# Batch statistics from second moments of the features, summed in the main loop

## The chip, the cores and the metric

The kernel runs on one core of a Trainium2 chip. The time is the device time of one execution in microseconds (us). The time before is the median of three runs. Five engines are named: PE (TensorE, matrix products), DVE (VectorE), ACT (ScalarE), POOL (GpSimd) and SP (SyncE, which here only issues transfers). Each takes its instructions in the order in which they are written, and waits at a semaphore until the count it asks for is reached; everything behind a waiting instruction on the same engine waits with it.

## The reference

The program takes x and ctx, both 32 x 128 x 1024. Four blocks follow each other: two chunked attentions with a layer norm, a graph block over the 30 nearest neighbours, and a third attention with a layer norm. Only the graph block matters here, cut to its first batch norm:

```python
idx = _knn(x_loc, k)                       # 30 neighbours of each of 32 x 1024 points
rel = pts[bidx, idx] - pts[:, :, None, :]
...                                        # rho, theta, phi: a radius and two angles
sph = jnp.stack([rho, theta, phi], axis=-1)
feat = jnp.concatenate([sph, sph - jnp.mean(sph, axis=-1, keepdims=True)], axis=-1)
lrelu = lambda h: jax.nn.leaky_relu(h, 0.2)
h = lrelu(_bn(feat @ W1.T, g1, b1))        # 6 channels, mean and variance over all rows
h = lrelu(_bn(h @ W2.T, g2, b2))           # 3 channels
h = lrelu(_bn(h @ W3.T, g3, b3))           # 1 channel
att = jax.nn.softmax(h[..., 0], axis=-1)
```

The first layer is linear in the three features, so its mean and variance over all 983,040 rows follow from the features' mean and their 3 x 3 matrix of second moments.

## The kernel before

There are three stages, one after the other, with a barrier between them.

**The main loop** (`attention_and_neighbours`) takes 32 batches in 24 steps each: 768 steps, and a tail of 48 steps in which only lagging work is left. In step s, PE makes the scores SC of step s (L581, L586), projections PJ for the next pass, distances PD (L599, L600), then the transposes PT of step s-3 (L607), the weighted values OP of step s-4 (L615), and fetches G of neighbours' coordinates (L558). DVE takes the scores' maximum (L1046), then reciprocals, and in pieces the search of neighbours: MAX8, MATCH_REPLACE8 and FIND_INDEX8 over rows of 1024. ACT makes the exponentials `prob` (L722) and copies PT and OP from PSUM (L729, L735). POOL divides `prob` by its sum (L835), splits rows (L813 to L823), masks and adds (L853, L860), selects coordinates (L924 to L927) and does the features of one batch (L937 to L977).

A second batch runs behind the first: everything with a name in `..._AT` happens so many steps after that batch's last step of attention, once in 24 steps. `ROOT_AT` is the radius on ACT (`sides`), `TURN_AT` and `SPH_AT` are the last steps of the two angles on POOL (L964; L975 and L977), and `SPH_OUT_AT` is the store of the three features by SP (L503, L505). The features of a batch are 128 partitions x 256, of which every 32nd and 31st partition are padding.

PE's scores of step s need ACT's exponentials of step s-2, since SC has two buffers:

```python
pe.wait_ge(exped, at_least(i, START + i * STEPS + s - 1, START))
```

**The batch norms** (`batch_norms`) load the features of all batches into `S` and run over them three times. In the first pass PE makes the first layer Z of each piece (L1258), and DVE takes its statistics (L1402):

```python
for y in range(2 * PIECES):
    dve.wait_ge(z1_ready, y + 1)
    dve.bn_stats(st1[:, y % 2, y // 2, :], Z[0:ROWS, y % BANKS, :]).then_inc(z1_read, 1)
```

PIECES is 60, so that is 120 products and 120 statistics. After it come an aggregate, two small products that average over the rows (`across`), an inverse root on POOL and `gain` and `shift`. The second pass makes the first layer again, for ACT to scale and shift it (L1327). `SERIAL` numbers the links of this chain.

**The weighted sum** (`neighbour_sum`) is not touched.

## Time and profile before

| | us |
|---|---|
| median of three runs | 6317.76 |
| lowest and highest | 6315.41, 6318.28 |
| the profiled execution's own time | 6316.55 |
| its span | 6314.8 |

| engine | busy, us | share of the span |
|---|---|---|
| PE | 5517.6 | 87% |
| DVE | 5699.2 | 90% |
| ACT | 4499.4 | 71% |
| POOL | 3397.5 | 54% |

The span begins with the main loop, which ends at about 4634 us; the batch norms end at about 5060 us. A share of busy time says which engine is full on average, not which wait ends last: that is read from the rows of a stretch in order of time. The trace shows a float32 product as two passes of PE (120 products are 240 rows), and a transpose as one.

### The profile page before, as it was taken

The page shows a single profiled execution, that of the slowest core. Times are in us where ns is not written, and L with a number is a line of the kernel's source. Part 1 is how long each engine was busy: PE and PEld are TensorE (multiplying, and loading weights), DVE is VectorE, ACT ScalarE, POOL GpSimd, SP SyncE. Part 2 cuts the span into 40 slices and gives each one's busy share as a digit, 9 for nine tenths or more (in the row PEclk, how much of TensorE's full clock was granted, in tenths as well). Part 3 has the DMA queues.
Part 4 walks back from the last instruction along what each step waited for, and adds up shares of the span by engine and source line. Part 5 has one row for each costly group of instructions (what it writes and reads, how often), then busy time and mean ns, then how long its engine had stood idle before and what let it go on. Part 6 is the DMA issues. An engine that isn't in the chain of part 4 may idle for free. (4 is left out here: it accounts for less than half of the span.)

```text
span 6314.8 us, 227176 instructions
## 1 busy us (share of the span) xinstructions
PE 5517.6 (87%) x82516; PEld 3384.3 (54%) x82516; DVE 5699.2 (90%) x8045; ACT 4499.4 (71%) x17145; POOL 3397.5 (54%) x3375
## 2 busy tenths in 40 slices
PE   7888888888888888888888888888669859999999
PEld 3555555555555555555555555555433347777776
DVE  7999999999999999999999999999855687777786
ACT  7888888888888888888888888888604623333333
POOL 3466666666666666666666666666620033333332
PEclk9999999999999999999999999999879979999999
DMA  2333333333333333333333333333340023333332
GB/s 45 95 105 97 99 98 96 95 95 107 98 110 91 99 98 96 97 97 109 96 107 93 97 97 97 97 108 92 106 108 0 0 64 89 94 87 88 84 94 74
DMA packets 651349, 568.72 MB, mean 90 GB/s; under 512 B 553072, under 2 KB 574832, under 8 KB 616208
## 3 DMA queue, kind: packets, MB, share of 16 engines
q1 hardware_dynamic: 613264, 284.51, 19.2%
q10 hardware_dynamic: 36864, 268.45, 12.0%
q8 instruction: 702, 11.50, 0.8%
q14 instruction: 519, 4.25, 0.2%
HBM read 384.76 MB, written 67.24 MB: 72 GB/s over the span
## 5 line engine op out<-in xcount | busy, mean ns | idle before, releaser
L722 ACT ACTIVATE prob<-SC,row_max 128x64 f32<-128x64 f32 x6144 | 1842.2, 337 | 389.7 <-DVE row_max L1046 381.6
L835 POOL TENSOR_TENSOR prob<-prob,row_rec 128x512 f32<-128x512 f32 x768 | 830.2, 1082 | 1433.5 <-DVE row_rec L1054 1403.5
L722 ACT ACTIVATION_READ_ACCUMULATOR prob<-SC,row_max 128x1 f32 x6144 | 1393.0, 230 | 0.0
L1038 DVE FIND_INDEX8 nbr<-top,dist 128x8 uint16<-128x1024 f32 x1024 | 1234.4, 1217 | 0.0
L1031 DVE MAX8 top<-dist 128x8 f32<-128x1024 f32 x1024 | 1190.8, 1203 | 1.7
L1033 DVE MATCH_REPLACE8 dist<-top,dist 128x1024 f32<-128x1024 f32 x768 | 923.3, 1206 | 0.0
L586 PE MATMUL SC<-k_bd,q_t 128*64 128x256 f32 x6144 | 907.1, 420 | 0.0
L1697 ACT ACTIVATE dense<-DM 128x512 f32<-128x512 f32 x512 | 305.6, 597 | 747.0 <-PE DM L1656 746.7
L607 PEld LDWEIGHTS PT<-ident,prob 128*128 128x128 f32 x3072 | 361.7, 145 | 833.8 <-issue 815.6
L1805 DVE TENSOR_TENSOR d_oh_a<-lo,iota_a 128x4096 bf16<-128x4096 bf16 x256 | 583.9, 2291 | 239.7 <-PE DM L1656 239.1
L607 PE MATMUL PT<-ident,prob 128*128 128x128 f32 x3072 | 490.9, 284 | 351.0 <-ACT prob_t L729 350.3
L558 PE MATMUL G<-table,low_all 128*128 128x24 bf16 x24576 | 706.0, 174 | 66.1 <-ACT picked L748 32.8
L558 PEld LDWEIGHTS G<-table,low_all 128*128 128x128 bf16 x24576 | 667.4, 97 | 177.5 <-issue 94.6
L1656 PEld LDWEIGHTS DM<-placed,d_oh_a 128*128 128x128 bf16 x24576 | 645.8, 96 | 111.4 <-issue 77.4
L1656 PE MATMUL DM<-placed,d_oh_a 128*128 128x32 bf16 x24576 | 651.4, 177 | 31.1 <-DVE d_oh_a L1805 28.2
L1046 DVE TENSOR_REDUCE row_max<-SC 128x8 f32<-128x512 f32 x768 | 518.6, 675 | 73.7 <-PE SC L586 73.3
L586 PEld LDWEIGHTS SC<-k_bd,q_t 128*64 128x64 f32 x6144 | 395.5, 144 | 316.5 <-issue 217.2
L600 PE MATMUL PD<-ctx 128*128 128x512 f32 x1024 | 542.1, 611 | 0.0
L729 ACT ACTIVATE prob_t<-PT 128x512 f32<-128x512 f32 x768 | 498.7, 649 | 0.4 <-PE PT L607 0.3
L1634 PE MATMUL AG<-dense,x_t 128*128 128x512 f32 x1024 | 476.5, 608 | 0.9 <-issue 0.7
L715 ACT ACTIVATE dist<-PD,xcol 128x512 f32<-128x512 f32 x512 | 372.1, 727 | 127.2 <-PE PD L600 111.2
L536 PE MATMUL PJ<-ctx,w_in 128*128 128x512 f32 x768 | 438.3, 653 | 0.1
(187 smaller groups left out, 9475.7 us busy)
## 6 DMA issues: line engine op xcount, KB each, us to landing
low_all<-low_scratch ACTq DMA_DIRECT2D x256, 1024.0 KB, 5.0
k_bd<-k_t SPq DMA_DIRECT2D x3072, 16.0 KB, 1.9
placed<-compact SPq DMA_DIRECT2D x256, 192.0 KB, 3.8
ctx<-in_ctx SPq DMA_DIRECT2D x32, 512.0 KB, 6.2
mask<-in_mask SPq DMA_DIRECT2D x32, 512.0 KB, 8.7
xb<-in_x SPq DMA_DIRECT2D x32, 512.0 KB, 3.3
x_scratch<-xb SPq DMA_DIRECT2D x32, 512.0 KB, 6.9
y_scratch<-y_b SPq DMA_DIRECT2D x32, 512.0 KB, 6.6
```

The source lines that it names most:

```text
L558: last = pe.matmul(G[:, g * 24:(g + 1) * 24], hot[:, t % 2, col:col + 128], table[:, v % BPB, part, :], start=(part == 0), stop=(part == 2))
L586: last = pe.matmul(bank[64 * ch:64 * ch + 64, cols], q_t[:, w % 2, here], k_bd[:, s // 2 % KEY_BUFS, s % 2 * 2 + ch, cols], start=False, s ...
L600: pe.matmul(PD[:, :], ctx[:, u, t * 128:(t + 1) * 128], ctx[:, u, h * HALF:(h + 1) * HALF], start=False, stop=True).then_inc(pd_ready, 1)
L607: last = pe.transpose(PT[:, m * 128:(m + 1) * 128], prob[:, r % 4, m * 128:(m + 1) * 128], ident[:, :])
L722: last = act.activation(prob[:, s % 4, g * CHUNK:(g + 1) * CHUNK], SC[:, s % 2, g * CHUNK:(g + 1) * CHUNK], ACT.Exp, bias=row_max[:, s % 2 ...
L835: pool.tensor_tensor(pr, pr, row_rec[:, r % 2, :].unsqueeze(2).to_broadcast([128, 8, CHUNK]), ALU.mult).then_inc(normed, 1)
L1031: dve.max(best, row).then_inc(top_step, 1)
L1033: dve.match_replace(row, best, row, NEG_BIG).then_inc(top_step, 1)
L1038: last = dve.max_index(nbr[:, uu % BPB, t, k * 8:(k + 1) * 8], best, row)
L1046: dve.tensor_reduce(row_max[:, s % 2, :], SC[:, s % 2, :].rearrange("p (h k) -> p h k", h=8), AX.X, ALU.max, negate=True).then_inc(maxed, 1)
L1656: last = pe.matmul(DM[:, x % DM_BANKS, (g % 16) * 32:(g % 16 + 1) * 32].rearrange("p (q m) -> p q m", q=4), oh_a[:, t % 2, g, :], placed[: ...
L1805: dve.tensor_tensor(oh_a[:, t % 2, :, :].rearrange("p g (a two) -> p g a two", two=2), lo2[:, u, t, :, :].unsqueeze(2).to_broadcast(wide), ...
```

## The change

It moves the first batch norm's statistics into the main loop.

- POOL writes `centred` for each batch (`CENTRE_AT` = 46): the three features side by side in 8 strips of 96 columns with a column of ones behind them; the radius has a typical value taken off, and padding rows are zero. That is a copy and three TENSOR_SCALAR instructions. It takes the space of `r2m`.
- PE adds to the 96 x 97 block `GR` in PSUM, over all batches, the product of each strip with itself: 8 float32 products in each batch (`GRAM_AT` = 47), ahead of OP in the same step. PE waits for `centre_ready` there. ACT copies the sum to SBUF once, at the end.
- `TURN_AT` goes from 45 to 44, `SPH_AT` from 46 to 45, and `SPH_OUT_AT` from 47 to 46. The radius is stored by itself, 39 steps behind, and SP loads one value of it into all partitions (`typical`, 42 steps behind).
- ACT waits for `centre_ready` of the batch before at the root, and POOL for `gram_ready` of the batch before at L948. Two POOL instructions lose an operation that multiplies by one.
- The first pass is gone: 120 products, 120 statistics, the aggregate and its two small products. In its place DVE makes mean and variance from `gram` with 18 small instructions before `gain`, and PE one product.

```diff
-RATIO_AT, ANGLE_AT, TURN_AT, SPH_AT, SPH_OUT_AT = 44, 44, 45, 46, 47
-TAIL = SPH_OUT_AT + 1
+RATIO_AT, ANGLE_AT, TURN_AT, SPH_AT, SPH_OUT_AT = 44, 44, 44, 45, 46
+RHO_OUT_AT, TYPICAL_AT, CENTRE_AT, GRAM_AT = 39, 42, 46, 47
+TAIL = GRAM_AT + 1
...
+                v = lagging(i, s, RHO_OUT_AT)
+                if v is not None:
+                    b = i * BPB + v
+                    sp.wait_ge(sides_ready, START + b + 1)
+                    alone(sp)
+                    sp.dma_start(dram["sph"][0][b], sides[:, 0, :]).then_inc(rho_out, 16)
+                v = lagging(i, s, TYPICAL_AT)
+                if v is not None:
+                    b = i * BPB + v
+                    sp.wait_ge(rho_out, START + 16)
+                    alone(sp)
+                    sp.wait_ge(centre_ready, START + b)
+                    alone(sp)
+                    sp.dma_start(typical[:, :], dram["sph"][0][0, TYPICAL:TYPICAL + 1, 0:1].broadcast_to([128, 1])).then_inc(typical_in, 16)
...
+            def products_of_features(i, s):
+                v = lagging(i, s, GRAM_AT)
+                if v is not None:
+                    pe.wait_ge(centre_ready, START + i * BPB + v + 1)
+                    for j in range(STRIPS):
+                        last = pe.matmul(GR[0:GRAM, 0:GRAM + 1], centred[:, j, 0:GRAM], centred[:, j, :], start=False, stop=True, skip_group_check=True)
+                    last.then_inc(gram_ready, 1)
...
                     pe.wait_ge(pt_ready, START + i * STEPS + r + 1)
                     pe.wait_ge(o_ready, START + i * STEPS + r)
+                    products_of_features(i, s)
                     for ch in range(2):
...
+                elif lagging(i, s, GRAM_AT) is not None:
+                    pe.wait_ge(o_ready, START + N * BSTEPS)
+                    products_of_features(i, s)
...
             all_steps(act, step)
+            act.wait_ge(gram_ready, START + N)
+            act.activation(gram[0:GRAM, :], GR[0:GRAM, 0:GRAM + 1], ACT.Identity).then_inc(gram_kept, 1)
+            act.wait_ge(gram_kept, START + 1)
...
+                    pool.wait_ge(gram_ready, START + b)
+                    alone(pool)
...
-                    pool.tensor_scalar(r2m[:, 0:3:2, :], r2[:, :, :], TINY, 1.0, ALU.max, ALU.mult).then_inc(r2_step, 1)
+                    pool.tensor_scalar(r2m[:, 0:3:2, :], r2[:, :, :], TINY, None, ALU.max).then_inc(r2_step, 1)
...
+                v = lagging(i, s, CENTRE_AT)
+                if v is not None:
+                    b = i * BPB + v
+                    pool.wait_ge(sides_ready, START + b + 1)
+                    alone(pool)
+                    pool.wait_ge(typical_in, START + (b + 1) * 16)
+                    alone(pool)
+                    pool.wait_ge(sph_ready, START + b + 1)
+                    alone(pool)
+                    pool.tensor_copy(centred[:, :, GRAM:GRAM + 1], real_rows[:, :].unsqueeze(1).to_broadcast([128, STRIPS, 1]))
+                    pool.tensor_scalar(centred[:, :, 0:STRIP], sides[:, 0, :].rearrange("p (j f) -> p j f", f=STRIP), typical[:, 0:1], real_rows[:, 0:1], ALU.subtract, ALU.mult)
+                    for c in range(2):
+                        last = pool.tensor_scalar(centred[:, :, (c + 1) * STRIP:(c + 2) * STRIP], angle[:, c, :].rearrange("p (j f) -> p j f", f=STRIP), real_rows[:, 0:1], 0.0, ALU.mult, ALU.add)
+                    last.then_inc(centre_ready, 1)
...
-            for y in range(2 * PIECES):
-                dve.wait_ge(z1_ready, y + 1)
-                dve.bn_stats(st1[:, y % 2, y // 2, :], Z[0:ROWS, y % BANKS, :]).then_inc(z1_read, 1)
```

On POOL, steps 45 and 46 of a batch's lag stand so before (`r` is `turn`):

```order
L927 TENSOR_TENSOR rel<-picked 128x32x3
L964 TENSOR_TENSOR r<-good,signs 128x256
L833 REGISTER_ALU
L835 TENSOR_TENSOR prob<-prob,row_rec 128x512
L823 CAST dist_row<-sq 32x1024
L824 REGISTER_ALU
L975 TENSOR_TENSOR angle<-angle,signs 128x256
L977 TENSOR_TENSOR angle<-angle,r 128x256
L833 REGISTER_ALU
L835 TENSOR_TENSOR prob<-prob,row_rec 128x512
```

and the same place on POOL in the changed kernel, whose lines have other numbers:

```order
L972 TENSOR_TENSOR rel<-picked 128x32x3
L1022 TENSOR_TENSOR angle<-angle,signs 128x256
L1024 TENSOR_TENSOR angle<-angle,r 128x256
L878 REGISTER_ALU
L880 TENSOR_TENSOR prob<-prob,row_rec 128x512
L868 CAST dist_row<-sq 32x1024
L869 REGISTER_ALU
L1030 ISA
L1034 COPY centred<-real_rows 128x8
L1035 TENSOR_SCALAR centred<-sides,typical,real_rows 128x8x32
L1037 TENSOR_SCALAR centred<-angle,real_rows 128x8x32 x2
```

The `turn` has gone a step up, the angle's two instructions stand where it was, and the copy and three TENSOR_SCALAR stand behind the CAST.

On PE, step 47 of the lag stands so before, from its scores SC to the fetch G:

```order
L581 MATMUL SC<-mask_row,two_chunks 128x512
L586 MATMUL SC<-k_bd,q_t 64x256 x4
L543 MATMUL PJ<-w_in,ctx 64x64 x16
L607 MATMUL PT<-ident,prob 128x128 x4
L615 MATMUL OP<-prob_t,v_b 32x64 x8
L554 REGISTER_ALU
L558 MATMUL G<-table,low_all 128x24 x48
```

and in the changed kernel, the same step on PE, with the next step's scores behind it:

```order
L618 MATMUL SC<-mask_row,two_chunks 128x512
L623 MATMUL SC<-k_bd,q_t 64x256 x4
L570 MATMUL PJ<-w_in,ctx 64x64 x16
L644 MATMUL PT<-ident,prob 128x128 x4
L596 MATMUL OP<-centred 96x97 x8
L653 MATMUL OP<-prob_t,v_b 32x64 x8
L581 REGISTER_ALU
L585 MATMUL G<-table,low_all 128x24 x48
L335 REGISTER_ALU
L615 REGISTER_ALU
L616 ISA
L618 MATMUL SC<-mask_row,two_chunks 128x512
```

The 8 products of strips stand between the transposes and the weighted values; the fetch and the next scores are behind them.

## Rows read from the trace of the kernel before

**Rows 1.** Busy time by engine in two stretches: main loop, first pass

```profile
core 0: us, PE busy (x) PEld busy (x) DVE busy (x) ACT busy (x) POOL busy (x), PEclk, DMA share, GB/s
146.00:4500.00 4354.00, 3847.33 (x53462) 2278.82 (x53462) 4276.57 (x6604) 3779.10 (x15722) 2798.79 (x2929) 0.95 0.35 99
4634.00:4760.00 126.00, 108.83 (x247) 41.50 (x248) 92.74 (x156) 0.00 (x0) 1.01 (x3) 0.91 0.45 95
```

**Rows 2.** DVE's maxima in order of time: start, duration, idle before

```profile
2117.51 0.69 DVE L1046 TENSOR_REDUCE row_max<-SC 128x8 f32<-128x512 f32 x1 [1.31 <-PE SC L586]
2125.69 0.68 DVE L1046 TENSOR_REDUCE row_max<-SC 128x8 f32<-128x512 f32 x1
2131.01 0.67 DVE L1046 TENSOR_REDUCE row_max<-SC 128x8 f32<-128x512 f32 x1
```

**Rows 3.** PE in order of time, the same stretch

```profile
2112.10 0.95 PE L607 MATMUL PT<-ident,prob 128*128 128x128 f32 x4 [2.62 <-ACT prob_t L729]
2112.98 0.65 PE L615 MATMUL OP<-prob_t,v_b 128*32 128x64 f32 x16
...
2119.09 0.66 PE L607 MATMUL PT<-ident,prob 128*128 128x128 f32 x4
2119.68 0.43 PE L615 MATMUL OP<-prob_t,v_b 128*32 128x64 f32 x16
...
2121.66 1.08 PE L586 MATMUL SC<-k_bd,q_t 128*64 128x256 f32 x8
```

**Rows 4.** POOL in order of time, the same stretch

```profile
2117.25 0.73 POOL L964 TENSOR_TENSOR r<-good,signs 128x256 f32<-128x256 f32 x1
2117.93 1.05 POOL L835 TENSOR_TENSOR prob<-prob,row_rec 128x512 f32<-128x512 f32 x1
2119.14 1.03 POOL L823 CAST dist_row<-sq 32x1024 bf16<-32x1024 f32 x1 [0.17 <-POOL prob L835]
2120.26 0.73 POOL L975 TENSOR_TENSOR angle<-angle,signs 128x256 f32<-128x256 f32 x1
...
2121.75 1.04 POOL L835 TENSOR_TENSOR prob<-prob,row_rec 128x512 f32<-128x512 f32 x1
```

**Rows 5.** POOL's groups by line, 146 to 4500 us: busy, mean ns, idle

```profile
L959 POOL TENSOR_TENSOR legs<-apart,good 128x512 f32<-128x512 f32 x30 | 38.4, 1279 | 0.0
L948 POOL TENSOR_SCALAR r2m<-r 128x512 f32<-128x512 f32 x30 | 58.1, 1937 | 5.9 <-POOL r L945 5.9
L951 POOL TENSOR_TENSOR r2m<-r2m,sqr 128x256 f32<-128x256 f32 x30 | 21.9, 728 | 2.4
L900 POOL CAST table<-pts 128x24 bf16<-128x24 f32 x31 | 6.3, 204 | 0.0
```

**Rows 6.** PE alone after idle times: stretch, length, busy, clock, DMA share, GB/s

```profile
2112.00:2119.00 7.00, 6.90 (x109) 0.52 0.33 136
4756.00:4764.80 8.80, 7.61 (x13) 0.52 0.00 0
```

**Rows 7.** The first pass and what follows, by engine, in order of time

```profile
4642.06 0.67 DVE L1397 TENSOR_SCALAR L<-bn_tables,w3c 96x32 f32<-96x32 f32 x4
4646.11 106.02 PE L1258 MATMUL Z<-sph_rows,L 96*96 96x512 f32 x240 [40.09 <-DMA sph_rows<-sph_scratch]
...
4756.37 0.48 PE L1265 MATMUL SUM<-mv,bn_tables 96*96 96x2 f32 x2 [4.24 <-DVE mv L1410]
...
4758.18 0.16 DVE L1419 COPY var<-SUM 96x2 f32<-96x2 f32 x1 [0.57 <-PE SUM L1267]
...
4760.11 0.77 ACT L1327 ACTIVATE h<-Z,shift,gain 96x512 f32<-96x512 f32 x1 [131.12 <-DVE shift L1423]
```

**Rows 8.** The main loop's tail: POOL, and SP's issues

```profile
4593.33 1.54 POOL L924 TENSOR_TENSOR picked<-picked,oh_b 128x768 f32<-128x768 f32 x1
...
4629.96 0.72 POOL L977 TENSOR_TENSOR angle<-angle,r 128x256 f32<-128x256 f32 x1
...
4634.11 0.34 SPq L1244 DMA_DIRECT2D bn_row<-in_bn_row  x1
```

**Rows 9.** Waits of DVE from 146 to 4500 us: total, times, longest

```profile
DVE row_max L1046 <- PE SC L586: 52.9, 49, 2.1
```

More of the change, by code:

```diff
@@ L763, in step @@
                     act.wait_ge(r2_ready, START + b + 1)
[L764 to L765 removed]
+                    act.wait_ge(rho_out, START + b * 16)
+                    act.wait_ge(centre_ready, START + b)
+                    act.activation(sides[:, 0:3, :], r2m, ACT.Sqrt).then_inc(sides_ready, 1)
                 v = lagging(i, s, ACROSS_AT)
@@ L1129 @@
 BANKS = 7
-SERIAL = ["weights"] + [f"{what}{n}" for n in (1, 2, 3) for what in ("local", "mean", "spread", "var_sum", "var", "inv", "gain")]
+SERIAL = ["weights", "second_moments", "pooled", "var1", "inv1", "gain1"]
+SERIAL += [f"{what}{n}" for n in (2, 3) for what in ("local", "mean", "spread", "var_sum", "var", "inv", "gain")]
+POINTS = N * T * K
 def batch_norms(nc, dram, keep):
-    att = keep["att"]
+    att, gram, typical = keep["att"], keep["gram"], keep["typical"]
     with ExitStack() as es:
@@ L1171, in batch_norms @@
         h1 = sb("h1", [ROWS, 3, 2, 512])
-        st1 = sb("st1", [ROWS, 2, PIECES, 6])
+        w1r = sb("w1r", [ROWS, 2, 3])
+        w1p = sb("w1p", [ROWS, 2, 3, 3])
+        pairs = sb("pairs", [ROWS, 3, N])
+        second = sb("second", [ROWS, 4])
+        own_second = sb("own_second", [ROWS, 3, 4])
+        pooled = sb("pooled", [ROWS, 3, 4])
+        centre = sb("centre", [ROWS, 3])
+        cov = sb("cov", [ROWS, 3, 3])
+        spread = sb("spread", [ROWS, 2, 3, 3])
+        along = sb("along", [ROWS, 2, 3])
         st2 = sb("st2", [ROWS, 1, PIECES, 6])
@@ new lines, in _ @@
+            dve.tensor_reduce(second[:, 0:3], pairs[:, :, :], AX.X, ALU.add)
+            link(dve.tensor_copy(second[:, 3:4], gram[0:ROWS, ROWS:ROWS + 1]))
+            mark(dve.tensor_tensor(own_second[:, :, :], second[:, :].unsqueeze(1).to_broadcast([ROWS, 3, 4]),
+                                   chan.unsqueeze(2).to_broadcast([ROWS, 3, 4]), ALU.mult))
+            wait(dve, "pooled")
+            link(dve.tensor_scalar(pooled[:, :, :].rearrange("p c x -> p (c x)"), SUM[0:ROWS, 0:12], 128.0 / POINTS, None, ALU.mult))
@@ new lines, in _ @@
+            link(dve.tensor_copy(centre[:, :], pooled[:, :, 3]))
+            link(dve.tensor_tensor(cov[:, :, :], centre[:, :].unsqueeze(2).to_broadcast([ROWS, 3, 3]), centre[:, :].unsqueeze(1).to_broadcast([ROWS, 3, 3]), ALU.mult))
+            link(dve.tensor_tensor(cov[:, :, :], pooled[:, :, 0:3], cov[:, :, :], ALU.subtract))
+            for half in range(2):
+                last = dve.tensor_tensor(spread[:, half, :, :], cov[:, :, :], w1r[:, half, :].unsqueeze(1).to_broadcast([ROWS, 3, 3]), ALU.mult)
@@ new lines, in _ @@
+            link(last)
+            link(dve.tensor_reduce(along[:, :, :], spread[:, :, :, :], AX.X, ALU.add))
+            link(dve.tensor_tensor(along[:, :, :], along[:, :, :], w1r[:, :, :], ALU.mult))
+            mark(dve.tensor_reduce(var[0:ROWS, :], along[:, :, :], AX.X, ALU.add))
+            link(dve.tensor_tensor(centre[:, 0:1], centre[:, 0:1], typical[0:ROWS, :], ALU.add))
+            link(dve.tensor_tensor(along[:, :, :], w1r[:, :, :], centre[:, :].unsqueeze(1).to_broadcast([ROWS, 2, 3]), ALU.mult))
@@ L1404, in norm @@
+            link(dve.tensor_reduce(mean[0:ROWS, :], along[:, :, :], AX.X, ALU.add))
             def norm(which, st, rows, width, g, b):
-                done, count = {1: (z1_read, 2 * PIECES), 2: (z2_seen, PIECES), 3: (z3_seen, PAIRS_K)}[which]
+                done, count = {2: (z2_seen, PIECES), 3: (z3_seen, PAIRS_K)}[which]
                 dve.wait_ge(done, count)
@@ L1919, in constants @@
     out["pow_half"] = np.full((128, 1), -0.5, np.float32)
+    out["real_rows"] = (np.arange(128) % KP < K).astype(np.float32).reshape(128, 1)
     out["turns"] = np.tile(np.array([SIGN_TIE, np.pi / 4], np.float32), (128, 1))
```

58 lines of the change are left out of this document (34 added, 24 removed).

## Prediction

> **What bounds the kernel now.** I read the busy time by stretch first, since the change gives in one stage and takes in another. In the main loop DVE is busy 4276.57 of 4354.00 us [rows 1]; of what is left, 52.9 us are 49 waits for the scores [rows 9]. So DVE sets the pace there, and an engine beside it costs nothing while its scores come before the maximum wants them. In the first pass of the batch norms PE is busy 108.83 of 126.00 us and DVE follows it [rows 1]; ACT stands idle all through it, 131.12 us, until `shift` [rows 7]. That pass is wholly on the path. Then I read three engines side by side, in order of time, at the one place of 24 steps where the change puts its work [rows 2 to 4]. The reader is to see there how late PE and POOL run against DVE: PE's scores for the maximum at 2125.69 end at 2121.66 + 1.08 = 2122.74, which leaves a slack of 2.95 us, and POOL goes from 2117.25 to 2122.8 with no pause.
>
> **What the first pass gives.** Before, ACT's second pass begins at 4760.11 [rows 7]. After, DVE is done with its weights at 4642.06 + 0.67 = 4642.7 as now, and a chain of small instructions follows. One of them takes 0.16, and DVE stands idle for 0.57 while PE makes a small product in between [rows 7]; with a gap I take 0.2 for each instruction and 0.7 for the trip through PE. Six instructions: 4643.9. Product and back: 4644.65. Nine of them start up to 4646.25, the last of which is `var`. From the start of `var` to ACT's start it is now 4760.11 - 4758.18 = 1.93; the three that make the mean lie beside POOL's root. ACT begins at 4648.2. PE's first product can begin at 4646.11 as now, when the features land, so it isn't later than that by more than its own pass. The gain is 4760.11 - 4648.2 = **112 us**. The loads of later pieces were fast enough for PE's 106.02 us [rows 7], and the second pass is slower than that, so they stay hidden. Ends: 105 (every small instruction twice as dear) and 114.
>
> **What POOL's step costs PE.** PE now waits ahead of OP for `centre_ready`. Before, OP begins at 2119.68 [rows 3]. POOL's chain in [rows 4], replayed: the selection ends at 2117.25. The angle's two instructions stand where `turn` was; they take 2121.75 - 2120.26 = 1.49, so `prob` begins at 2118.74. From `prob` to the CAST 1.21, from the CAST to what follows 1.12: 2121.07. The copy of 128 x 8 is priced by the CAST of 128 x 24, 0.204 [rows 5], with a gap 0.28. The three TENSOR_SCALAR of 128 x 256 have no row. The one of 128 x 512 takes 1.937; two-input instructions take 1.279 for 512 and 0.728 for 256, so about 0.18 is fixed [rows 5], and half of the rest makes 0.18 + 0.88 = 1.06, with a gap 1.14. Three are 3.42. `centre_ready` comes at 2121.07 + 0.28 + 3.42 = **2124.8**, and PE is held 5.1 us. Ends: 0.73 each as a two-input instruction (2123.8), and 1.94 each as the whole row of 512 (2127.4). The value is near the lower end since size halves.
>
> The row says that one input and two operations are dearer than two inputs. The Trainium skill says the opposite of a plain case: "GPSIMD Engine Reference", section 4.1 "Engine selection", has one-input elementwise work at roughly line rate and two-input work about twice as slow as on DVE. By that rule the three would cost less than 0.73 each, which would lead to the second rival below; this case's trace has 1.937 against 1.279 and disagrees.
>
> **What the products cost.** 8 float32 products are 16 passes of 96 weights and 97 columns. The nearest row is a pass with 128 weights and 128 columns: four take 2119.68 - 2119.09 = 0.59 at full clock and 2112.98 - 2112.10 = 0.88 after an idle time [rows 3], 0.15 and 0.22 each. Ends: 0.02 (16 narrow passes of OP in 0.36) and 0.44 (240 passes of 512 columns in 106.02 us) [rows 3, 7].
>
> **The clock.** In this same step of the loop the granted clock stands at 0.52 for the 7 us from 2112 to 2119, its lower level of 1.2 GHz, after PE had stood idle for 2.62 us; it does so again for 8.8 us behind the first pass, where PE waited 4.24 us for the aggregate [rows 3, 6, 7]. PE was busy for 106.02 us before that second idle time, as it is busy before the hold. A hold of 5.1 us is longer than both, so I take the lower level from 2124.8 to about 2131.8. Then the products take 16 x 0.22 = 3.5: 2128.3. From OP's start to the maximum of the next scores it takes 2122.74 - 2119.68 = 3.1 at full clock and 2117.51 - 2112.98 = 4.5 at the lower one [rows 2, 3]; 3.5 of those 4.5 pass before 2131.8, and the last 1.0 halves. The scores are there at **2132.3**.
>
> **What DVE waits.** 2132.3 - 2125.69 = 6.6 us in each batch. Behind the waiting maximum stand DVE's search instructions, which can't go ahead. After it the next maximum is due 5.3 us later (2131.01 against 2125.69) [rows 2]; PE's rows replayed from 2132.3 put its scores 1 us ahead of that, and those of the one behind it half a us ahead, so nothing more is lost and nothing is won back: DVE is full. The next scores of PE, the fetch G, ACT's copy of OP and its exponentials stand in the same queue. The hold comes in 29 batches: the products of the 30th fall in the last of 768 steps, with no maximum behind, and those of the last two in the tail. 29 x 6.6 = **191 us**. Ends: 29 x 1.2 = 35 (cheap POOL, narrow passes, full clock) and 29 x 13 = 377 (all three upper ends).
>
> **The tail.** It is a chain through POOL, so what is added stands on the path. For the last batch, POOL ends at 4630.68 and the next stage begins at 4634.11, after SP's stores [rows 8]. Now POOL's 3.7, the products 3.5 and ACT's copy with its waits about 0.8 take the place of those 3.4: +4.6. For the batch before, PE has its products ahead of the second half of the fetch for the selection at 4593.33 [rows 8]; 3.7 + 3.5 and the fetch and copy behind them make about +10, less if POOL's pace is all that counts (+3.7). Together **+15**, from 8 to 18.
>
> **Edits that cost nothing.** SP's store of the radius waits for ACT's root, with the key copies of steps 40 and on behind it; those are wanted four steps later, some 23 us (4354 us are 740 steps of 5.9). The load of `typical` is one value 128 times, four steps ahead of POOL's use. ACT's wait for `centre_ready` and POOL's for `gram_ready` ask for the batch before, more than ten steps old. `turn` one step up falls in an idle time of POOL. The dropped multiplications on POOL can only save, at a place where POOL isn't waited for.
>
> **The sum**, against the profiled execution's 6316.55: -112 + 191 + 15 = +94, which makes **6411**. The median of the runs is 1.2 higher; that is noise here, and a measurement of this kernel can tell about 0.2%, 13 us, from no change.
>
> **Rivals.**
> 1. The clock holds. Products 2.4, from OP to the maximum 3.1: scores at 2130.3, a wait of 4.6, 133 in all; with a tail of 13 the time is 6351. Against it stand both stretches of [rows 6]; for it, that these are two idle times of other lengths behind other work.
> 2. POOL is cheap and the new work nearly fits the slack: TENSOR_SCALAR at 0.73, products at 2.4 or less, full clock. Scores at 2123.8 + 2.0 + 3.1 = 2128.9 or earlier, a wait of 1.7 to 3.2, 50 to 93 in all; with a tail of 8 it is 6263 to 6306, so 6285: **faster**. It decides at a wait of (112 - 8) / 29 = 3.6 us: above that the loop takes more than the pass gave. This is the result by the skill's rule on POOL.
> 3. The work is hidden altogether, since POOL isn't as late in most batches as in the one I read: -112 + 8 makes 6213. Against it: a batch is 24 steps of the same instructions, and the 49 waits of [rows 9] are about what two places in 31 batches would make.
> 4. Everything is dearer: TENSOR_SCALAR at 1.5 and more, weights that don't load beside the products. A wait of 10 makes 290, and 6510 and above.
> 5. The change doesn't do what it says, for instance features that land too late for the second pass to start early: against it, PE's one wait for them ends at 4646.11 [rows 7].
>
> **Chances.** Forecast 0.57, holds-the-clock 0.18, nearly-fits 0.10, hidden 0.04, dearer 0.10, the fifth 0.01 (it falls among the slower). Faster by over 0.2% is most of the second and the third, 0.12; within 0.2% is what of the first two lies near 3.6 us, 0.04; slower 0.84. The range takes in the forecast with its ends at waits of 5.5 and 9, and the first rival, and reaches to 6315 and 6495; that leaves out the hidden case, most of the second rival and part of the fourth, 0.19.
>
> **What would show it.** In the profile after: a wait of DVE's maximum for PE's scores, once in 24 steps, 29 times, of 5.5 to 8 us (190 us more than the 52.9 of now); ahead of PE's first strip product an idle time of 5 us that ends with POOL's last TENSOR_SCALAR; that instruction at 1.06; the products at 3.5 and a clock of 0.5 behind the hold; DVE's busy time in the loop unchanged; ACT's second pass 14 us after the stage's start. A POOL that reaches the centring before PE reaches OP would make the forecast wrong at its root; a TENSOR_SCALAR below 0.8 with a full clock would make it wrong in size and perhaps in sign.

## The result and the profile after

The changed kernel takes **6466.49 us** (median of 4 runs, 6461.28 to 6482.7); the kernel before takes 6316.59 us on the same chip (6311.62 to 6318.28). The ratio is **1.0243**, with a 95% interval from 1.0223 to 1.0263: slower by 2.4%. The forecast was 6411, within 6315 to 6495.

The profiled execution has a span of 6459.4 us, against 6314.8 before. Where it is spent can be read from SyncE's first DMA of each stage. This is the timeline of SP of the kernel after: start and duration in us, then the engine's queue, line and tiles.

```profile
4837.14 0.34 SPq L1315 DMA_DIRECT2D bn_row<-in_bn_row  x1
...
5177.71 0.34 SPq L1657 DMA_DIRECT2D d_ident<-in_ident  x1
```

| stage | before | after | difference | forecast |
|---|---|---|---|---|
| main loop and tail | 4634.11 | 4837.14 | +203.0 | +206 |
| batch norms | 453.5 | 340.6 | -112.9 | -112 |
| neighbour sum | 1227.2 | 1281.7 | +54.5 | 0 |

Before, the last stage begins at 5087.56 (later than the 5060 named above). So two stages came out as forecast, and the third, whose code the change doesn't touch, lost 54.5 us that no step of the prediction has.

**Main loop.** DVE's waits from 146 to 4500 us (total, times, longest), the view of [rows 9]:

```profile
DVE row_max L1107 <- PE SC L623: 221.2, 78, 10.9
```

The wait for the scores is 221.2 us in place of 52.9. It isn't one wait of 6.6 us in each batch, though. These are DVE's maxima behind two successive sets of products; the number in brackets is the idle time just before, and what ended it:

```profile
2070.11 0.69 DVE L1107 TENSOR_REDUCE row_max<-SC 128x8 f32<-128x512 f32 x1 [10.95 <-PE SC L623]
...
2215.75 0.69 DVE L1107 TENSOR_REDUCE row_max<-SC 128x8 f32<-128x512 f32 x1 [2.58 <-PE SC L623]
```

All through the trace the two sizes alternate. Of DVE's waits of more than 2.4 us there are 29 in the main loop, with 180.4 us in all: 13 where the loop jumps back, of 7.9 to 10.95 us, 127.5 together, and 16 others of 2.6 to 5.0, 52.9 together. PE's timeline at the jump shows why (the answer to [rows 3]):

```profile
2051.65 0.63 PE L644 MATMUL PT<-ident,prob 128*128 128x128 f32 x4 [0.31 <-ACT prob_t L771]
2057.22 2.87 PE L596 MATMUL OP<-centred 128*96 128x97 f32 x16 [4.94 <-POOL centred L1037]
2060.02 0.66 PE L653 MATMUL OP<-prob_t,v_b 128*32 128x64 f32 x16
2060.61 1.46 PE L585 MATMUL G<-table,low_all 128*128 128x24 bf16 x48
2067.55 0.60 PE L618 MATMUL SC<-mask_row,two_chunks 64*128 64x512 bf16 x1 [5.49 <-issue]
```

PE is held 4.94 us for POOL, the 16 passes take 2.87, and then, behind the fetch G, PE stands idle for another 5.49 us that nothing in the data explains. "issue" is time in which the engine waits for nothing that the profile shows. Between G and SC stands the branch back to the top of the loop. In the kernel before the same gap is there, 3.53 us:

```profile
1977.14 1.37 PE L558 MATMUL G<-table,low_all 128*128 128x24 bf16 x48
1982.04 0.38 PE L581 MATMUL SC<-mask_row,two_chunks 64*128 64x512 bf16 x1 [3.53 <-issue]
```

It stands at all 13 jumps of the loop, 3.45 to 3.98 us before and 3.85 to 5.49 after. The jump shown has the longest hold and the longest gap: over the 13 jumps the hold is 2.8 to 4.94 us, 4.1 on average. The group of the products has all idle time ahead of them from 146 to 4500 us (busy us, mean ns, idle before):

```profile
L596 PE MATMUL OP<-centred 128*96 128x97 f32 x448 | 79.4, 370 | 100.9 <-POOL centred L1037 71.3 <-ACT prob_t L771 29.6
```

That is 28 sets of 16 passes, so 3.6 us of hold for each.

Before, PE comes to the jump without the 4.94 + 2.87 us of the hold and the products, and most of the gap lies in its slack; DVE waits 1.01 us for it:

```profile
1984.23 0.69 DVE L1046 TENSOR_REDUCE row_max<-SC 128x8 f32<-128x512 f32 x1 [1.01 <-PE SC L586]
```

In the middle of the body, one batch later than the jump shown, the hold is shorter and there is no second gap:

```profile
2206.19 0.66 PE L644 MATMUL PT<-ident,prob 128*128 128x128 f32 x4
2209.83 2.87 PE L596 MATMUL OP<-centred 128*96 128x97 f32 x16 [2.98 <-POOL centred L1037]
2212.64 0.43 PE L653 MATMUL OP<-prob_t,v_b 128*32 128x64 f32 x16
2213.00 1.37 PE L585 MATMUL G<-table,low_all 128*128 128x24 bf16 x48
```

The granted clock of PE behind the two holds (stretch, length, PE busy, clock, DMA share, GB/s):

```profile
2057.20:2072.50 15.30, 9.79 (x94) 0.50 0.18 49
2209.80:2217.00 7.20, 7.17 (x95) 0.81 0.27 84
```

At the jump it stays at 1.2 GHz, its lower level, for the whole 15.3 us. In the middle it comes back within the stretch: OP takes 0.43 and G 1.37 already, as they do at full clock.

POOL's timeline at the jump (the answer to [rows 4]) and, under it, its groups for the two forms of the centring (busy us, mean ns, idle before):

```profile
2053.33 1.03 POOL L868 CAST dist_row<-sq 32x1024 bf16<-32x1024 f32 x1 [0.17 <-POOL prob L880]
2054.74 0.20 POOL L1034 COPY centred<-real_rows 128x8 f32<-128x8 f32 x1 [0.38 <-POOL dist_row L868]
2054.93 1.23 POOL L1035 TENSOR_SCALAR centred<-sides,typical,real_rows 128x256 f32<-128x256 f32 x1
2056.13 0.94 POOL L1037 TENSOR_SCALAR centred<-angle,real_rows 128x256 f32<-128x256 f32 x2
```

```profile
L1035 POOL TENSOR_SCALAR centred<-sides,typical,real_rows 128x256 f32<-128x256 f32 x28 | 34.4, 1228 | 0.0
...
L1037 POOL TENSOR_SCALAR centred<-angle,real_rows 128x256 f32<-128x256 f32 x56 | 26.3, 481 | 0.0
```

**Batch norms.** DVE's chain and ACT's start, in the order of [rows 7]:

```profile
4847.75 0.17 DVE L1473 TENSOR_SCALAR pooled<-SUM 96x12 f32<-96x12 f32 x1 [0.65 <-PE SUM L1341]
...
4849.23 0.15 DVE L1482 TENSOR_REDUCE var<-along 96x2 f32<-96x6 f32 x1
```

```profile
4836.47 0.25 ACT L832 ACTIVATE gram<-OP 96x97 f32<-96x97 f32 x1 [7.15 <-PE OP L596]
4851.23 1.60 ACT L1392 ACTIVATE h<-Z,shift,gain 96x512 f32<-96x512 f32 x2 [14.52 <-DVE shift L1511]
```

ACT begins its pass 4851.23 - 4837.14 = 14.1 us into the stage, as against 126.0 before.

### The profile page after: what moved, and what is told of

Its sections match the earlier page's. It is cut to its first block and busy times, and to the rows that moved or that the text cites. A ratio compares the mean times of both kernels' runs of the same rounds, so it can differ in the third digit from the quotient of the medians.

```text
span 6459.4 us, 228016 instructions
## 1 busy us (share of the span) xinstructions
PE 5528.3 (86%) x82788; PEld 3447.8 (53%) x82788; DVE 5622.4 (87%) x7936; ACT 4492.6 (70%) x17146; POOL 3427.3 (53%) x3503
## 5 line engine op out<-in xcount | busy, mean ns | idle before, releaser
L880 POOL TENSOR_TENSOR prob<-prob,row_rec 128x512 f32<-128x512 f32 x768 | 800.6, 1042 | 1595.5 <-DVE row_rec L1115 1595.4
L637 PE MATMUL PD<-ctx 128*128 128x512 f32 x1024 | 556.1, 625 | 0.0
L1722 PE MATMUL AG<-dense,x_t 128*128 128x512 f32 x1024 | 490.1, 623 | 0.7 <-issue 0.7
```

The costliest lines, as they stand in the source:

```text
L637: pe.matmul(PD[:, :], ctx[:, u, t * 128:(t + 1) * 128], ctx[:, u, h * HALF:(h + 1) * HALF], start=False, stop=True).then_inc(pd_ready, 1)
L880: pool.tensor_tensor(pr, pr, row_rec[:, r % 2, :].unsqueeze(2).to_broadcast([128, 8, CHUNK]), ALU.mult).then_inc(normed, 1)
L1722: last = pe.matmul(AG[:, hh, :], x2_t[:, u, m, :], dense[hh][:, m, :], start=(m == 0), stop=(m == 7))
```

## Experiments

All times below are of profiled executions. The "main loop" ends with SP's first DMA of the batch norms, and it takes in the tail of the features. One profile has noise: the same kernel, run as e5_away_from_jump and as e9_step_50, ended its main loop at 4688.65 and at 4699.18. Differences under some 12 us in that column tell nothing.

| kernel | main loop ends | batch norms | neighbour sum | whole |
|---|---|---|---|---|
| before | 4634.1 | 453.5 | 1227.2 | 6316.6 |
| after | 4837.1 | 340.6 | 1281.7 | 6461.3 |
| e1_moved_tiles | 4638.2 | 452.7 | 1229.9 | 6322.6 |
| e2_early_operand | 4705.1 | 341.0 | 1273.1 | 6321.0 |
| e3_step_later | 4711.0 | 340.3 | 1228.7 | 6281.8 |
| e4_same_place | 4842.8 | 340.4 | 1233.7 | 6418.7 |
| e5_away_from_jump | 4688.7 | 338.8 | 1230.0 | 6259.2 |
| e6_top_in_place | 4697.6 | 338.6 | 1226.6 | 6264.6 |
| e7_jump_in_place | 4708.5 | 338.2 | 1229.4 | 6277.8 |
| e8_before_shifted | 4634.9 | 453.2 | 1288.0 | 6378.0 |
| e9_step_50 | 4699.2 | 339.8 | 1227.7 | 6268.5 |
| e10_one_early_product | 4677.4 | 339.9 | 1247.7 | 6266.7 |
| e11_one_held_product | 4782.1 | 339.8 | 1242.9 | 6366.7 |
| e12_centre_earlier | 4738.2 | 339.2 | 1286.2 | 6365.5 |

### Who takes 54 us from a stage that wasn't changed?

Two things of the neighbour sum move with the change: the addresses of its tiles (two small tiles stand ahead of all others now), and the place of its code in PE's instruction stream. Here is the top of the loop's body in PE's timeline, first before, then after:

```profile
5482.44 1.96 PE L1643 MATMUL XT<-d_ident,d_x 128*128 128x128 f32 x8 [3.57 <-issue]
5484.20 2.77 PE L1656 MATMUL DM<-placed,d_oh_a 128*128 128x32 bf16 x96
```

```profile
5664.47 1.97 PE L1731 MATMUL XT<-d_ident,d_x 128*128 128x128 f32 x8 [4.08 <-issue]
5666.23 0.32 PE L1744 MATMUL DM<-placed,d_oh_a 128*128 128x32 bf16 x4
5668.60 2.63 PE L1744 MATMUL DM<-placed,d_oh_a 128*128 128x32 bf16 x92 [2.05 <-issue]
```

The transposes XT stand first behind the jump, then come 96 passes DM. After the change four of these go, and then PE idles for 2.05 us "issue". That gap comes in all 13 passes of the loop, with 2.03 to 2.76 us in 12 of them and 1.75 in one. In the middle of the body PE also waits for the DMA of `placed`, 12 times with 15.1 us in all, which it didn't before. The gaps are 28.0 of the 54.5 us and these waits 15.1; the rest isn't assigned.

**e1_moved_tiles**: the kernel before, with only the addresses moved.

```diff
         keep = {}
+        keep["gram"] = es.enter_context(nc.sbuf_tensor("gram", [128, 97], F32))
+        keep["typical"] = es.enter_context(nc.sbuf_tensor("typical", [128, 1], F32))
         attention_and_neighbours(nc, dram, keep)
```

> The kernel before, with nothing changed but two SBUF tiles of 97 and 1 f32 columns allocated ahead of all others, as the change does; nothing reads or writes them. The neighbour sum's stage, whose code the change leaves alone, took 1227.2 us before and 1281.7 after. If the moved addresses are the cause, it takes about 1282 here and the whole about 6371. If they are not, it stays at 1227 and the whole at 6316. The main loop ends at 4634 in either case.

The stage took 1229.9 us. Addresses are out.

**e4_same_place**: the changed kernel, with PE instructions added ahead of the stage's loop, in a stretch where PE waits for data.

```diff
             pe.wait_ge(consts_in, START + 16 * len(CONSTS))
+            for _ in range(71):
+                pe.matmul(AG[:, 0, 0:8], ident[:, :], ident[:, 0:8], start=True, stop=True)
+            pe.transpose(AG[:, 0, 0:128], ident[:, :], ident[:, :])
```

> The changed kernel with 71 small products and one transpose of the identity on PE at the start of the neighbour sum, where PE waits 22 us for its first blocks anyway. They replace the PE instructions that the change took out ahead of that stage, so that the stage's loop stands where it stood in PE's instruction stream before. Theory: PE fetches its code in pieces, and where the loop stands against them sets what it idles behind the jump; then the stage is back from 1281.7 to about 1227 us, the gap of 2.05 us some four products behind the jump is gone, and the whole is at about 6412. Rival: it is the address of tiles, or a queue of DMAs; then the stage stays at 1282 and the whole at 6466.

The stage is back at 1233.7 us, and all 96 passes DM run as one:

```profile
5583.26 1.56 PE L1734 MATMUL XT<-d_ident,d_x 128*128 128x128 f32 x8 [3.60 <-issue]
5584.61 2.75 PE L1747 MATMUL DM<-placed,d_oh_a 128*128 128x32 bf16 x96
```

**e8_before_shifted** is the reverse, and the stronger one, since it has nothing of the change in it: the kernel before with 56 such products and the transpose.

```diff
             pe.wait_ge(consts_in, START + 16 * len(CONSTS))
+            for _ in range(56):
+                pe.matmul(AG[:, 0, 0:8], ident[:, :], ident[:, 0:8], start=True, stop=True)
+            pe.transpose(AG[:, 0, 0:128], ident[:, :], ident[:, :])
```

> The kernel before, with 56 small products and a transpose on PE ahead of the neighbour sum, where PE waits 22 us anyway: its loop moves back by 226 PE instructions, which is where the change puts it (286 forward) if the pieces are 256 long. Theory of the code's place: the neighbour sum takes about 1282 us in place of 1227, with a second gap of 2 us some four products behind the transposes at the top of each body, and the whole 6371, with nothing of the change in it. Rival: the 54 us are tied to something else that the change does: the stage stays at 1227 and the whole at 6316.

The stage took 1288.0 us, and the gap stands behind the fourth pass, as in the kernel after:

```profile
5497.82 1.97 PE L1646 MATMUL XT<-d_ident,d_x 128*128 128x128 f32 x8 [3.50 <-issue]
5499.58 0.31 PE L1659 MATMUL DM<-placed,d_oh_a 128*128 128x32 bf16 x4
5501.68 2.64 PE L1659 MATMUL DM<-placed,d_oh_a 128*128 128x32 bf16 x92 [1.78 <-issue]
```

So the place of PE's code is the cause, shown in both directions. The other runs fill in the rule. I counted the PE instructions ahead of this loop in the built programs (four for a float32 product, which is two passes of a weight load and a matmul; two for a product of one pass; one for a wait or a branch), and took what differs from the kernel before modulo 256 (the remainder after whole pieces of 256). The PE instructions of the traces give the same differences:

| place, modulo 256 | kernels | neighbour sum |
|---|---|---|
| 0 | before, e1, e4 | 1227.2, 1229.9, 1233.7 |
| 2 or 3 | e3, e5, e6, e7, e9 | 1226.6 to 1230.0 |
| 56, 58 | e10, e11 | 1247.7, 1242.9 |
| 224 | e2 | 1273.1 |
| 226 | after, e8, e12 | 1281.7, 1288.0, 1286.2 |

The gap itself moves as it should if the code comes in pieces of 256 instructions and a border of pieces stands at the loop's top in the kernel before. With e2, two instructions (one pass) fewer stand ahead of the loop, and the gap is one pass later, behind the fifth:

```profile
5530.27 1.97 PE L1730 MATMUL XT<-d_ident,d_x 128*128 128x128 f32 x8 [4.03 <-issue]
5532.02 0.34 PE L1743 MATMUL DM<-placed,d_oh_a 128*128 128x32 bf16 x5
5534.36 2.61 PE L1743 MATMUL DM<-placed,d_oh_a 128*128 128x32 bf16 x91 [2.00 <-issue]
```

With e10 the border would stand 3297 (the body's instructions) + 56 - 13 x 256 = 25 instructions ahead of the body's end, which is the branch and 12 passes. There it is, 1.06 us, in five of the 13 passes:

```profile
5486.50 4.68 PE L1743 MATMUL DM<-placed,d_oh_a 128*128 128x32 bf16 x180
5492.24 0.47 PE L1743 MATMUL DM<-placed,d_oh_a 128*128 128x32 bf16 x12 [1.06 <-issue]
5496.29 1.96 PE L1730 MATMUL XT<-d_ident,d_x 128*128 128x128 f32 x8 [3.59 <-issue]
```

In the other eight the gap is missing, and the idle time at the jump itself is 4.05 to 5.00 us in place of 3.59 to 3.88.

The traffic of the code can be seen in the page's DMA queues (packets, MB, share of 16 engines). This is the line of the kernel before, and under it that of e8:

```profile
q8 instruction: 702, 11.50, 0.8%
```

```profile
q8 instruction: 716, 11.73, 0.8%
```

The kernel after has 723. All these packets have 16,384 bytes. Counted from the start of the neighbour sum, there are 220 or 221 of them in the ten kernels without the gap near the top of the body, and 233 or 234 in the four with it (after, e2, e8, e12): 13 more, one for each pass of the loop.

The Trainium skill has the size: "Advanced Engine Details and Errata", section "ISA Cache", gives the instruction cache lines of 16 KB, 256 instructions. The runs agree with that figure. The same page's section "Control Flow Timing" has a branch at about 51 ns, and about 108 ns with a compare; in these traces PE stands idle for 3.1 us and more at every jump of a loop as long as these, so those figures don't tell what such a jump costs.

The trace shows the fetch, too. In each of the 13 gaps of the kernel after, a packet of q8 ends 1.34 to 1.66 us before PE goes on, and at each of its jumps in this stage one ends 1.63 to 1.83 us before; over the whole run q8 has one packet in some 9 us. A packet doesn't say which engine it is for. That PE waits for it is inferred from this timing, from the count of 13 and from the gap's place.

### What in the products costs the main loop 203 us?

**e2_early_operand**: the products read the identity and wait for nobody (the sums are not those of the features).

```diff
-                    pe.wait_ge(centre_ready, START + i * BPB + v + 1)
                     for j in range(STRIPS):
-                        last = pe.matmul(GR[0:GRAM, 0:GRAM + 1], centred[:, j, 0:GRAM], centred[:, j, :], ...
+                        last = pe.matmul(GR[0:GRAM, 0:GRAM + 1], ident[:, 0:GRAM], ident[:, 0:GRAM + 1], ...
```

> The changed kernel, but the 16 passes of the feature products read the identity, which is there from the start, and wait for nothing, so the first batch norm's statistics are not the reference's; GpSimd still centres. Theory: what the main loop loses (203 us) is PE's hold for the centring (111.7 us of idle in the trace, up to 4.9 a batch), which puts PE behind by more than its slack, and at every second batch stands right before the loop's jump, whose 3.5 to 5.5 us of PE idle then add to it. Without the hold the main loop ends near 4650 to 4710 instead of 4837, and the whole is at about 6280 to 6340. Rival: the products themselves, in the stream of PE, are the loss (2.87 us at 1.2 GHz): then the loop ends above 4780.

The loop ended at 4705.1, within what was expected: 132 of the 203 us were the hold and what it drags along. Some 121 of them lie before the last maximum (4593.4 against 4714.6) and 11 in the tail.

**e10_one_early_product** is the same with `range(1)` in place of `range(STRIPS)`, which leaves out seven eighths of the sums.

```diff
-                    for j in range(STRIPS):
+                    for j in range(1):
                         last = pe.matmul(GR[0:GRAM, 0:GRAM + 1], ident[:, 0:GRAM], ident[:, 0:GRAM + 1], ...
```

> e2_early_operand with one product of the identity (2 passes) in place of eight (16), so that seven eighths of the sums are left out. The main loop ended at 4705 with eight, 71 later than before. If the products in PE's stream are that, 14 passes fewer of 0.11 us at 2.4 GHz to 0.18 at 1.2 GHz give back 1.6 to 2.5 us a batch, 45 to 70 in all, and it ends at 4635 to 4660. If it is the centring on GpSimd, or the features' tail behind the last batch, it ends at 4700 still.

It ended at 4677.4, 28 us earlier, less than the 45 to 70 expected if the products were all the rest, and more than none. Some 43 us are left for one product and the centring on POOL. None of it is the tail, since the last maximum already begins 45 us later than before (4565.6 against 4520.9). I didn't split them further.

**e11_one_held_product** keeps the hold and leaves out seven eighths of the sums: `range(1)` in the changed kernel.

```diff
                     pe.wait_ge(centre_ready, START + i * BPB + v + 1)
-                    for j in range(STRIPS):
+                    for j in range(1):
```

> The changed kernel with one product of the centred features in place of eight (the sums of seven strips are left out); PE waits for the centring as before. Theory: the hold does the damage, up to 4.9 us a batch and the jump behind it, the eight products add 2.87 - 0.4 = 2.5 us a batch once PE is late: the main loop ends near 4837 - 30 x 2.5 = 4762, still 128 later than before. Rival: the products alone are the loss, and it ends near 4650; or the hold alone, and it stays at 4830.

It ended at 4782.1, 55 earlier than the kernel after and 148 later than before, where the theory had 4762 and 128. Both rivals, with a single cause each, fall; the hold weighs most. In the middle of the body PE still waits as long:

```profile
1890.46 0.61 PE L596 MATMUL OP<-centred 128*96 128x97 f32 x2 [2.85 <-POOL centred L1037]
```

So leaving out seven of the products gives 28 us where PE comes in time, and 55 where it has been held and runs at the lower clock. Not all of it is the products: the shorter body also moves the loop's jump, and the idle time there is 0.7 us shorter on average in e10 than in e2, and 0.8 in e11 than in the kernel after (see e7), which is up to 9 and 11 us over 13 jumps.

**e12_centre_earlier** centres one step earlier.

```diff
-RHO_OUT_AT, TYPICAL_AT, CENTRE_AT, GRAM_AT = 39, 42, 46, 47
+RHO_OUT_AT, TYPICAL_AT, CENTRE_AT, GRAM_AT = 39, 42, 45, 47
```

> The changed kernel with the centring one step earlier on GpSimd (45 in place of 46), the products left at 47. The centring then stands ahead of one division of prob (1.04 us) and one cast (1.03 us) and ends some 2.5 us earlier: PE's hold falls from 4.9 to some 2.5 us at the jump and from 2.9 to 0.4 in the middle of the body. Theory: the loop ends between e2_early_operand and the changed kernel, near 4740. Rival: the division that is pushed back by 2.4 us reaches PE's transposes late, and the loop ends at 4800 or more. The neighbour sum stays at 1273 to 1288 in either case, since PE's code does not move.

It ended at 4738.2, as expected. At nine of the 13 jumps PE's timeline shows no hold at all and at one 0.33 us, and the products at 1.54 us in place of 2.87, but the gap behind them stays (at the other three PE was held 2.5 us still):

```profile
2015.95 1.06 PE L644 MATMUL PT<-ident,prob 128*128 128x128 f32 x4
2016.85 1.54 PE L596 MATMUL OP<-centred 128*96 128x97 f32 x16
2018.31 0.43 PE L653 MATMUL OP<-prob_t,v_b 128*32 128x64 f32 x16
2018.68 1.37 PE L585 MATMUL G<-table,low_all 128*128 128x24 bf16 x48
2025.25 0.60 PE L618 MATMUL SC<-mask_row,two_chunks 64*128 64x512 bf16 x1 [5.20 <-issue]
```

DVE's waits behind the jumps are 4.6 to 5.6 us there, and 6.5 to 8.0 behind those three. The rival with the late division of `prob` would have had the loop at 4800 or more.

**e3_step_later** moves the consumer, not the producer.

```diff
-RHO_OUT_AT, TYPICAL_AT, CENTRE_AT, GRAM_AT = 39, 42, 46, 47
+RHO_OUT_AT, TYPICAL_AT, CENTRE_AT, GRAM_AT = 39, 42, 46, 48
...
-                    pe.wait_ge(centre_ready, START + i * BPB + v + 1)
+                    pe.wait_ge(centre_ready, START + i * BPB + v + 2)
...
+            pool.memset(centred[:, :, :], 0.0).then_inc(centre_ready, 1)
```

> The changed kernel with the products one step later (48 in place of 47), so that the centring has a whole step to be done; one extra product of zeros stands ahead of the first batch, and the waits count one more. Theory of the hold: PE no longer waits for the centring, the products cost some 1.8 us at 2.4 GHz inside PE's slack, and the loop ends near 4640 to 4690; the whole is then at about 6230 (if the neighbour sum is back at 1227) to 6320. Rival: the products now stand just behind the jump, in the step where PE is late already, and every second batch still loses 4 us or more: the loop ends at 4700 or later.

It ended at 4711.0, where the rival had put it (4700 or later), but the whole is at 6281.8: faster than before by 0.6%. DVE's maxima behind the jump show what the rival meant, a second wait 7 us behind the first. It is 1.9 to 2.2 us at four of the 13 jumps, and 0.7 to 1.3 at the others:

```profile
2010.82 0.69 DVE L1108 TENSOR_REDUCE row_max<-SC 128x8 f32<-128x512 f32 x1 [2.86 <-PE SC L623]
...
2018.26 0.69 DVE L1108 TENSOR_REDUCE row_max<-SC 128x8 f32<-128x512 f32 x1 [2.04 <-PE SC L623]
```

**e5_away_from_jump** has all else as e3.

```diff
-RHO_OUT_AT, TYPICAL_AT, CENTRE_AT, GRAM_AT = 39, 42, 46, 48
+RHO_OUT_AT, TYPICAL_AT, CENTRE_AT, GRAM_AT = 39, 42, 46, 50
```

> The products at step 50 in place of 48, all else as in e3_step_later (281.. 288.3 us a loop body there, from 1723.07 to 3164.41 in five; 283.4 in the kernel before). Theory: in e3 the products of every second batch stand in the step just behind the jump, where PE is late already, and VectorE waits a second time, 2.0 to 2.2 us (at 2018.26, 2308.18, 3171.91). Two steps later PE has its slack again: that wait goes, and the main loop ends about 14 x 2 = 28 us earlier than 4711, near 4683; the whole is at about 6252. Rival: the slack is as thin at any step, the wait only moves, and the loop ends at 4711 again.

(The 288.3 us in that text are the length of a body in e3.) The second wait is gone or small (0.8 us at most); the first stays, with 1.0 to 4.0 us. Here it stands alone:

```profile
2292.03 0.69 DVE L1108 TENSOR_REDUCE row_max<-SC 128x8 f32<-128x512 f32 x1 [2.08 <-PE SC L623]
```

Twelve bodies take 286.7 us each. The loop ended at 4688.7, and the same kernel's second profile at 4699.2. So the gain over e3 is between 12 and 22 us, not much above the noise.

**e6_top_in_place** and **e7_jump_in_place** asked whether the place of the code sets the main loop's gap, too. They put 63 or 47 small products ahead of PE's first work, and 1 or 17 ahead of the neighbour sum.

```diff
+            for _ in range(63):
+                pe.matmul(GR[0:GRAM, 0:4], v_b[:, 0, 0, 0:GRAM], v_b[:, 0, 0, 0:4], start=True, stop=True)
             pe.matmul(GR[0:GRAM, 0:GRAM + 1], v_b[:, ...
```

> e5_away_from_jump with 63 small products on PE ahead of its first work, and 1 ahead of the neighbour sum. They put the top of the main loop 256 of PE's instructions behind its place in the kernel before (it was 4 behind), and the neighbour sum's loop 2 behind. PE idles 4.7 to 5.2 us at the main loop's jump in e3_step_later and 3.5 to 3.75 before. Theory A: the place of the loop's top against the pieces in which code is fetched (256 instructions, if the shift of 254 in e3_step_later counts as 2) sets that: the idle is back at 3.6 and a body 1 to 1.5 us shorter than in e5. Theory B: it is the place of the jump itself, or the work queued ahead of it: nothing changes at the jump. The start of the kernel is some 10 us later in either case.

> e5_away_from_jump with 47 small products ahead of PE's first work, and 17 ahead of the neighbour sum: the main loop's jump now stands 256 PE instructions behind its place in the kernel before (it was 68 behind), its top 192, the neighbour sum's loop 2. Theory B: the place of the jump sets the idle behind it: it is back at 3.6 us, and a body 1 to 1.5 us shorter than in e5. Theory A: the top counts, and it now stands elsewhere: the idle stays at 5 us or grows, or a second gap opens some products behind the top.

Over all 13 jumps PE idled 4.64 us on average in e5, 4.27 in e6, 3.74 in e7 and 3.65 in the kernel before. With the top of the loop back in its place (e6) the gap isn't back. Theory B holds for the idle time: with the jump back in its old place, so is the gap, 3.44 to 4.06 us at every jump. But the second gap of which theory A speaks is there as well. In e7 PE idles once more behind each of the 13 jumps, 0.35 to 1.19 us, in the middle of the scores' products:

```profile
2018.91 1.54 PE L623 MATMUL SC<-k_bd,q_t 128*64 128x256 f32 x5
2020.89 1.12 PE L623 MATMUL SC<-k_bd,q_t 128*64 128x256 f32 x3 [0.43 <-issue]
```

No other kernel's trace has it. What neither brings is time: bodies took 286.7, 286.1 and 287.0 us in e5, e6 and e7, against 283.3 before.

All 14 traces sort by the place of this jump, again counted in PE's instructions from its place in the kernel before, modulo 256. A packet of q8 ends in the gap at every jump. At 0 or 12 (before, e1, e7, e8, e10, e11) it is one at every jump, and the gap is 3.4 to 4.25 us. From 64 to 69 (after, e2 to e6, e9, e12) it is one at some, with 3.5 to 4.7 us, and two at the others, with 4.6 to 5.5. Why a second packet comes at some jumps and not at others, the traces don't tell. In the kernel after nine of the 13 jumps have two, and so a part of its main loop's loss, 1.1 us for each jump and some 14 at most, is an effect of the code's place and not of the hold.

**e9_step_50** is e5 word for word, timed.

> e5_away_from_jump again, word for word, timed in five rounds against the kernel before. Theory: the change is worth its gain of 112 us in the batch norms once its products wait for nobody and stand away from the jump, and the neighbour sum's loop stands well in PE's code: 6259, a ratio of 0.990 (0.988 to 0.992). Rival: the one look at e5 was a lucky one; the ratio's interval takes in 1.0.

The median is **6264.1 us** (4 runs, 6252.31 to 6268.83) against 6318.48 (7 runs, 6314.44 to 6321.84), a ratio of **0.9909**, 95% interval 0.9893 to 0.9926. This version beats both kernels, the one before by 0.9% and the changed one by some 3%. It is the change with its products three steps later, one product of zeros ahead and the waits' counts one higher. That this puts the neighbour sum's loop 2 modulo 256 from its old place, and not 226, is luck, and part of the gain.

## Why the prediction was right, and where it was not

**What the first pass gives: right.** -112.9 for -112. Nine small instructions and a trip through PE ended with `var` at 4849.23, 12.1 us into the stage, and the forecast had 12.1 as well (4646.25 - 4634.11).

**What POOL's step costs PE: too much by 1.5 us.** The forecast had a hold of 5.1 us in every batch, and it was 3.6 on average. At the jump shown it is 4.94, near the forecast by two errors that cancel. The three TENSOR_SCALAR take 1.23 and twice 0.47, not three times 1.06: the form with two pointers is dear, the form with a pointer and a number is less than half of what the row of 512 columns led to. The centring takes 2.4 us, not 3.7; and it begins 2.46 us behind the time at which OP would begin (2054.74 against 2052.28), not 1.4. In the middle of the body it begins 0.5 us behind it (2207.36 against 2206.85), and the hold is 2.98.

The rule weighed there, the Trainium skill's "GPSIMD Engine Reference", section 4.1 "Engine selection", with one input cheaper than two, holds in this trace for the form with one pointer (0.481 us for 256 columns against 0.728 for two tensors [rows 5]), and not for the form with two (1.228). Together the four instructions cost what the second rival had for them, 2.4 us against 0.28 + 3 x 0.73 = 2.5.

**The products: 2.87 us for 3.5** at the lower clock, 1.54 where the clock was not down (e12). Between the bounds, a little high.

**The clock: right at the jump, wrong in the middle.** The forecast had 1.2 GHz for 7 us from the end of every hold. At the jump it was 0.50 for 15.3 us, where a second idle time followed; behind the shorter hold in the middle it was up again within 3 us. How much of the 132 us is the clock and how much the hold can't be said, since no run could hold the one without the other.

**What DVE waits: the sum right, the step wrong.** Up to the last maximum the loop took 4714.56 - 4520.94 = 193.6 us more, for 191 forecast. The sum is right by luck. The step that failed is "a batch is 24 steps of the same instructions", by which one place was read and multiplied by 29. The loop's body is 48 steps, and every second set of products stands right ahead of the jump, whose 3.5 us of idle PE had been hidden by PE's lead. The 29 waits that were forecast are there, but 13 of them have 9.8 us on average and 16 have 3.3; the mean, 6.2, is near the 6.6 forecast by chance. The hold is shorter than forecast, and the 3.9 to 5.5 us of the jump, which the sum lacks, stand behind every second one. Read as two places the prediction would have seen that the same work three steps later meets a PE with its slack, and there the change gains (e5, e9).

**The tail: +9.4 for +15**, within its ends of 8 and 18: from the last maximum to the stage's end, 4837.14 - 4714.56 = 122.6 in place of 113.2.

**The neighbour sum: the missing 55 us.** The forecast had nothing there, since nothing of it changes. This is the term that failed in size: 0 forecast, 54.5 measured. With it the sum would be 6465.5, against 6461.3 of the profiled execution; the other 4 us are the main loop's and the batch norms'. The prediction counted what an instruction costs, and not what it does to the code behind it. The range held the time because it had been widened for a dearer main loop; the reason was another.

**The rivals.** The clock came back early in half of the places, as in the first rival, but the loss of the main loop is the forecast's all the same. The second rival describes the middle of the body: POOL at its price, and waits of 3.3 us on average, where it had 1.7 to 3.2. The jump is what it lacks. With the products three steps later e9's 6264 lies within the 6263 to 6306 of that rival, though by another road than cheap instructions.

## What to carry to other kernels

A loop's jump is a place of its own on an engine with a long body: look for the "issue" gap behind it, and put no wait and no extra work on that engine just ahead of it. When a stage that wasn't touched changes its time, compare the gaps "issue" behind its jump, and the number of instruction packets on the page, before you look at its data; some tens of filler instructions, in a stretch where that engine waits anyway, move the code and tell. Work that is added for a slack has to be placed where its operand is ready: here the same 16 passes, three steps later, end the main loop 138 to 148 us earlier. The kernel went from 2.4% slower to 0.9% faster, and 52 to 54 us of that are the neighbour sum's code, which fell in a better place by chance.

## What the runs showed of the hardware

PE idled 3.1 to 5.5 us at every jump back over a body of some 7400 (main loop) or 3297 instructions (neighbour sum), and a packet of 16,384 bytes of the instruction queue ended 1.35 to 3.0 us before it went on. Where a border of 256 instructions stood shortly behind the top of the second, 1.73 to 2.76 us of idle were added in each pass, and PE's waits for `placed` with them: 1273 to 1288 us for the stage in place of 1227 to 1234, with 13 more packets for 13 passes. On POOL a TENSOR_SCALAR of 128 x 256 took 1.228 us with two pointer operands and 0.481 with a pointer and a number.
